# Gate products of an mLSTM block: from two column groups of 64 to four of 32

## The reference

```
xn    = layernorm(x)                       # (512, 512) per sequence
q,k,v,o = xn @ Wq.T, xn @ Wk.T, xn @ Wv.T, xn @ Wog.T
i_pre = 15 * tanh((xn @ Wig.T + big) / 15) # 8 heads: input gate
f_pre = 15 * tanh((xn @ Wfg.T + bfg) / 15) # 8 heads: forget gate
# scan over the tokens, per head:
f_log = log_sigmoid(f_pre)
m_new = max(f_log + m, i_pre)
C, n  = exp(f_log + m - m_new) * (C, n) + exp(i_pre - m_new) * (k v^T, k)
h     = (q C) / max(|q n|, exp(-m_new))
y     = x + (sigmoid(o) * headnorm(h)) @ Wout.T
out   = y + gelu(layernorm(y) @ ternary(w1).T + b1) @ ternary(w2).T + b2
```

## Time and profile before

| what | value |
|---|---|
| median of three runs | 1802.89 us (1798.72 to 1803.27) |
| the profiled execution's own time | 1799.08 us |
| its span, first to last instruction | 1797.3 us |
| TensorE busy | 1750.3 us (97% of the span) |
| VectorE busy | 1374.1 us (76%) |
| ScalarE busy | 1069.2 us (59%) |
| GpSimd busy | 588.2 us (33%) |
| mean granted clock of TensorE | 0.990 of full speed |

### The profile page before, as it was taken

How to read it: one execution, slowest core, us unless ns; L and a number is a source line. 1 busy time by engine, 2 the same in 40 slices (tenths; PEclk the granted TensorE clock), 3 DMA queues, 4 the chain that set the end, 5 groups by cost and what they waited for, 6 DMA issues and landing times.

```text
span 1797.3 us, 32014 instructions
## 1 busy us (share of the span) xinstructions
PE 1750.3 (97%) x12544; PEld 875.8 (49%) x12544; DVE 1374.1 (76%) x2464; ACT 1069.2 (59%) x1801; POOL 588.2 (33%) x481
## 2 busy tenths in 40 slices
PE   5879999999999999999999999999999999999999
PEld 3454544445454444545444454444544444454555
DVE  6787878787777778877877887877778787876772
ACT  5877648374663837557383754737466483746643
POOL 1241432524234252432425143252414325242340
PEclk8899999999999999999999999999999999999999
DMA  8434133251322425142252514325142342514020
GB/s 288 168 100 111 46 100 86 54 145 32 114 54 80 119 48 150 25 121 54 54 144 48 134 29 120 66 54 145 36 126 46 98 92 54 121 28 124 1 53 24
DMA packets 233525, 156.97 MB, mean 87 GB/s; under 512 B 195088, under 2 KB 199312, under 8 KB 228256
## 3 DMA queue, kind: packets, MB, share of 16 engines
q1 hardware_dynamic: 231792, 151.79, 31.8%
q10 hardware_dynamic: 1584, 3.15, 0.5%
HBM read 90.48 MB, written 17.24 MB: 60 GB/s over the span
## 4 chain that ended last, share of the span: by engine, by line
PE 91%; DVE 3%; ACT 1%; issue 1%; POOL 1%; DMA 0%; POOLq 0%; DVEq 0%; ACTq 0%
PE pf L1986 24%; PE pf L1970 23%; PE pa L1829 20%; PE pa L1805 9%; PE psh L1829 6%; PE psh L1926 2%; PE psh L1887 1%; PE psh L1910 1%; PE pa L1796 1%; PE psh L1960 1%; PE psh L1868 1%; PE pa L1926 1%; PE psh L1843 1%; DVE kT L1468 0%; ACT dec L930 0%
## 5 line engine op out<-in xcount | busy, mean ns | idle before, releaser
L1986 PE MATMUL pf<-w2T,gT 128*128 128x512 f16 x2048 | 497.1, 379 | 0.0
L1970 PE MATMUL pf<-x2T,w1T 128*128 128x512 f16 x1920 | 422.0, 379 | 0.0
L1970 PEld LDWEIGHTS pf<-x2T,w1T 128*128 128x128 f16 x1920 | 185.4, 98 | 222.6
L1522 DVE SCALAR_TENSOR_TENSOR gT<-g,wscale,gT 128x512 f16<-128x512 f32 x240 | 212.2, 884 | 105.6 <-ACT gT L966 105.0
L1986 PEld LDWEIGHTS pf<-w2T,gT 128*128 128x128 f16 x2048 | 195.3, 97 | 176.4
L1829 PE MATMUL pa<-wT,xT 128*128 128x512 f16 x960 | 213.5, 380 | 1.0 <-ACT sig L889 0.9
L963 ACT ACTIVATE g<-pf,b1c 128x512 f32<-128x512 f32 x240 | 164.0, 683 | 75.7 <-PE pf L1970 73.5
L971 ACT ACTIVATE ktok<-kT 128x512 f32<-128x512 f32 x64 | 40.4, 631 | 260.4 <-DVE kT L1446 260.4
L966 ACT ACTIVATE gT<-g,wscale 128x512 f16<-128x512 f32 x240 | 173.3, 722 | 7.8
L1829 PE MATMUL pa<-wT,shared 128*128 128x512 f16 x768 | 176.2, 379 | 0.8 <-DMA shared<-qT 0.7
L1805 PE MATMUL pa<-xT,wT 128*128 128x512 f16 x768 | 171.3, 379 | 0.1
(11 more groups left out here) (230 smaller groups left out, 2666.5 us busy)
## 6 DMA issues: line engine op xcount, KB each, us to landing
dec<-gate_r SPq DMA_DIRECT2D x32, 1024.0 KB, 5.6
xin<-L_attn_x SPq DMA_DIRECT2D x16, 1024.0 KB, 6.2
out<-x1b SPq DMA_DIRECT2D x64, 256.0 KB, 2.2
xres<-L_attn_x SPq DMA_DIRECT2D x16, 512.0 KB, 5.9
xres<-L_attn_x SPq DMA_DIRECT2D x32, 256.0 KB, 2.9
qw<-gate_w SPq DMA_DIRECT2D x128, 48.0 KB, 5.6
gT<-L_ffn_w SPq DMA_DIRECT2D x5, 1024.0 KB, 4.8
gT<-L_ffn_w ACTq DMA_DIRECT2D x3, 1024.0 KB, 6.2
```

What stands on the lines that cost most here:

```text
L1522: nc.vector.scalar_tensor_tensor(gT[:, LO, f, :], g32[:, f % 2, :], wscale[:, W_GELU:W_GELU + 1], gT[:, HI, f, :], ALU.mult, ALU.subtract) ...
L1970: last = nc.tensor.matmul(bank, w1T[:, k, tok(f)], x2T[:, part, :, k, :], start=(k == 0 and part == HI), stop=(k == KD - 1 and part == LO))
L1986: last = nc.tensor.matmul(bank, gT[:, part, f, tok(t)], w2T[:, f, :], start=(f == 0 and part == HI), stop=(f == NF - 1 and part == LO), sk ...
```

## The change

- The gate products go to four column groups of 32 PSUM partitions, one for each depth block. The twelve matmuls stay, of 32 weight columns instead of 64. The forget gate is in columns 0 to 7 now and the input gate in columns 8 to 15 (GROWS = 16).
- There are four partial sums in place of two: ScalarE copies the last, VectorE adds three others one after the other, each waiting for the one before; the third frees the bank.
- The input gate's rows of `th` are brought to partitions 0 to 7 (`gi`) by a new transfer of 16 KB on SyncE's queue, and VectorE multiplies them by 15 there, after a new wait, in `gate_decay`; the multiplication in `gate_logs` goes.
- On SyncE's queue the store of `ge` (and its wait for ScalarE's L866) stands behind the two large `dec` transfers now, not ahead of them.
- `gate_columns` stands behind the first query product on TensorE, and behind the first query copy on ScalarE.

```diff
-    GATE_F = 32
-    GROWS = GATE_F + NH
+    GROWS = 2 * NH
+    QUAD = P // KD
...
-        wgT = sb("wgT", [P, KD, 2, P // 2], F16)
+        wgT = sb("wgT", [P, KD, 2, QUAD], F16)
...
             def gate_rows(b):
+
+                sp.wait_ge(tanh_ok, at(b, 1, 1))
+                sp.dma_start(gi, th[NH:GROWS, :]).then_inc(i_loaded, 16)
                 sp.wait_ge(r_ok, at(b, 1, 1))
                 sp.dma_start(gate_r[b], th[0:NH, :]).then_inc(r_stored, 16)
-                sp.wait_ge(gate_act, at(b, 5, 4))
-                sp.dma_start(gate_w[b], ge[:, 0:LATE]).then_inc(w_stored, 16)
...
                     sp.dma_start(dec[:, g * H4:(g + 1) * H4, :],
...
+                sp.wait_ge(gate_act, at(b, 5, 4))
+                sp.dma_start(gate_w[b], ge[:, 0:LATE]).then_inc(w_stored, 16)
                 sp.wait_ge(w_stored, at(b, 16, 16))
...
-                nc.scalar.activation(th, pa[P // 2:P // 2 + GROWS, pa_bank(b, U_GATE), :], ACT.Copy).then_inc(gate_lo, 1)
+                nc.scalar.activation(th, pa[3 * QUAD:3 * QUAD + GROWS, pa_bank(b, U_GATE), :], ACT.Copy).then_inc(gate_lo, 1)
...
                     keys(b, 1)
+                    queries(b, 0)
                     gate_columns(b)
-                    queries(b, 0, 1)
+                    queries(b, 1)
...
             def gate_sum(b):
 
+                bank = pa_bank(b, U_GATE)
                 dve.wait_ge(gate_lo, at(b, 1, 1))
-                nc.vector.tensor_tensor(th, pa[0:GROWS, pa_bank(b, U_GATE), :], th,
-                                        ALU.add).then_inc(pa_free[pa_bank(b, U_GATE)], 1)
+                nc.vector.tensor_tensor(th, pa[2 * QUAD:2 * QUAD + GROWS, bank, :], th, ALU.add).then_inc(gate_part, 1)
+                dve.wait_ge(gate_part, at(b, 2, 1))
+                nc.vector.tensor_tensor(th, pa[QUAD:QUAD + GROWS, bank, :], th, ALU.add).then_inc(gate_part, 1)
+                dve.wait_ge(gate_part, at(b, 2, 2))
+                nc.vector.tensor_tensor(th, pa[0:GROWS, bank, :], th, ALU.add).then_inc(pa_free[bank], 1)
...
-                nc.vector.tensor_scalar(gi, th[0:NH, :], CAP, None, ALU.mult)
-                nc.vector.tensor_scalar(gf, th[GATE_F:GROWS, :], CAP, 0.0, ALU.mult, ALU.min)
+                nc.vector.tensor_scalar(gf, th[0:NH, :], CAP, 0.0, ALU.mult, ALU.min)
...
+                dve.wait_ge(i_loaded, at(b, 16, 16))
+                nc.vector.tensor_scalar(gi, gi, CAP, None, ALU.mult)
                 dve.wait_ge(gate_arg, at(b, 3, 3))
...
-                for k in range(KD // 2):
-                    for n, (ws, xs) in enumerate(PARTS):
-                        for half, rows_of in enumerate((slice(0, P // 2), slice(P // 2, P))):
-                            kc = 2 * k + half
-                            last = nc.tensor.matmul(bank[rows_of, :], wgT[:, kc, ws, :], xT[:, xs, :, kc, :],
-                                                    start=(k == 0 and n == 0), stop=(k == KD // 2 - 1 and n == 2))
+                for n, (ws, xs) in enumerate(PARTS):
+                    for k in range(KD):
+                        last = nc.tensor.matmul(bank[k * QUAD:(k + 1) * QUAD, :], wgT[:, k, ws, :], xT[:, xs, :, k, :],
+                                                start=(n == 0), stop=(n == 2), skip_group_check=True)
...
                 for n in range(HG):
                     features(b, U_K + n, C_QK + QK + n * P)
                     prepare(USES_O[n + 2])
-                gate_columns(b)
                 for n in range(HG):
                     features(b, U_Q + n, C_QK + n * P)
+                    if n == 0:
+                        gate_columns(b)
```

More of the change, by code:

```diff
@@ L254, in block_program @@
         gate_lo, tanh_ok = sem("gate_lo"), sem("tanh_ok")
+        gate_part, i_loaded = sem("gate_part"), sem("i_loaded")
         gate_arg = sem("gate_arg")
@@ L452, in _ @@
                     sp.wait_ge(s_const, 1)
[L453 to L456, removed]
+                    sp.dma_start(th[0:NH, :], Wfg).then_inc(s_wload[4], 16)
+                    sp.dma_start(th[NH:GROWS, :], Wig).then_inc(s_wload[4], 16)
+                    sp.dma_start(gate_bias[0:NH, :], bfg.unsqueeze(1)).then_inc(s_bias, 16)
+                    sp.dma_start(gate_bias[NH:GROWS, :], big.unsqueeze(1)).then_inc(s_bias, 16)
             sp.dma_start(gcol[:, :], gamma.rearrange("h v -> (h v)").rearrange("(k p) -> p k", p=P),
@@ L1295, in gate_minus @@
                     dve.wait_ge(hoT_loaded[T - 1], at(b, 16, 0))
-                nc.vector.tensor_scalar(ge, th[GATE_F:GROWS, :], CAP, None, ALU.mult).then_inc(gate_arg, 1)
+                nc.vector.tensor_scalar(ge, th[0:NH, :], CAP, None, ALU.mult).then_inc(gate_arg, 1)
                 dve.wait_ge(gate_arg, at(b, 3, 1))
```

## The result

The changed kernel takes 1804.74 us (median of 20 runs, 1802.52 to 1807.96); the kernel before, run beside it on the same chip, 1801.78 us (20 runs). The ratio is 1.0021, 95% interval 1.0014 to 1.0027: 3.8 us slower, which is also the distance of the means (1805.19 and 1801.37 us); the medians lie 3.0 apart. The 3.8 us are inside the predicted range, but I had forecast no change, and the interval excludes none. The profiled execution has a span of 1802.6 us, against 1797.3 before.

The account below looks back on a forecast made before the run. In steady blocks TensorE's queue alone was taken to bound the kernel. 1799.1 - 1.0 (steady blocks) + 0.7 (block 0) = 1798.8 profiled, 1802.6 against the runs' median; own range 1798 to 1807, wider range 1796 to 1814.

Parts of the forecast that it names:

- The gate products: Twelve matmuls on TensorE: four column groups side by side take 0.77 us instead of 1.42, a gain of 0.65.
- The sums: VectorE's three dependent sums make TensorE wait at `project(b, 3)`: 0.07 us gain left per block, 1.0 over 15 blocks.
- the 0.4 to 0.6 that I had named as a sign: TensorE's wait for VectorE's last sum, some 0.4 to 0.6 us in each of 15 blocks, if the forecast was right.
- VectorE's later work and `gate_columns`: VectorE's chain after the sums: r about 0.8 us later; `gate_columns`, done 0.1 us late behind a query product, costs 0.
- The store of `ge`: On SyncE's queue behind `dec`: lands at 1010.9; first query copy at 1011.6 leaves the output gate 0.3 us slack, cost 0.
- The second rival: The store of `ge` behind `dec` holds up the queries: 0.7 us a block, 10.5 in all, 1813 us; chance 0.12.
- The transposing transfer: On SyncE's queue, lands at 1021.6 before the first `up` product's weight load at 1022.15: slack 0.5 us, cost 0.
- The rival: The transposing transfer is late for the first `up` product: 1.0 us a block, 1818 us; chance 0.10.
- block 0: The first block, where TensorE waits for others: VectorE's two added sums cost 0 to 1.4 us once, taken as 0.7.
- "Cost 0": The new transfer of the input gate: some 4 us from issue to use against 1.40 for a small store, cost 0.

Follow-up runs that it names:

- e4: The changed kernel with the store of `ge` ahead of `dec` again and token tile 1's value product ahead of tile 0's: 1795.98 us, ratio 0.9973.
- e6: e4 with ScalarE's first key copy ahead of its token copies: 1792.92 us, ratio 0.9955 to the kernel before.
- e9: e1 with `gate_columns` back ahead of both query products, on TensorE and ScalarE: 1810.09 us, ratio 1.0042.
- e1: The changed kernel with the store of `ge` back ahead of the `dec` transfers: 1800.54 us, ratio 0.9999 to the kernel before.
- e2: The kernel before with only the store of `ge` moved behind the `dec` transfers: 1802.31 us, ratio 1.0005.
- e3: The changed kernel with the value product of token tile 1 moved ahead of that of tile 0: 1804.56 us, ratio 1.0020.
- after: The changed kernel itself, with the whole change and no further edit: 1804.74 us, ratio 1.0021 to the kernel before.
- e10: The kernel before with tile 1's value product first, the key copy first and `gate_columns` behind the first query product: 1801.86 us, ratio 1.0006.
- e7: e6 with block 0's transfer of the input gate issued by ScalarE instead of SyncE: 1792.08 us, ratio 0.9952.

## Why the prediction was wrong, point by point

**The gate products: right.** Forecast 0.77 us, measured 0.76 (e4, e6). Three steps of 0.216 are 0.65; the other 0.11 were there with two groups too (1.42 - 1.30). The Trainium skill's page TensorE: Matmul & The Clock Gate, Part 3, gives 2.38 times for three groups, from which I had estimated 0.9; here four groups are nearer to their ideal than that. My reason for leaving that figure aside did not hold, though: L1868 at 17 ns instead of 27 shows that its products overlap, but 27 / 17 is only 1.6 times, and I had no row for what one such float32 product costs alone.

**The sums: right in size.** Forecast were 0.07 us a block left over and a period of 106.2 to 106.3; it is 106.21. The sums step by 0.72 (991.36, 992.08, 992.80) and end 3.74 us behind `project(b, 2)`, forecast 3.7. The wait for the last sum is 0.2 us a block, not the 0.4 to 0.6 that I had named as a sign, because TensorE has already lost time just before it. This I had not seen: the value product waits as well, 0.16 us in most blocks, since it takes the bank of `project(b, 2)`, which L1489 frees. It costs nothing, because the next product waits for the sums anyway. This agrees with the rule cited from the Trainium skill (TensorEngine Tiling (Array Packing), PSUM Bottleneck): the products got faster, the emptying of the bank did not, and e4 and e6 give the time back once another product stands in between.

**VectorE's later work and `gate_columns`: right.** r is stored 0.7 us later (15.47 us behind the gate products against 14.80), forecast 0.8, and `gate_columns` costs nothing where the change put it. e9 shows what the move is worth.

**The store of `ge`: right.** The `qw` transfers, which wait for it, go out 24.05 us behind the gate products (1013.72 - 989.67); forecast 1010.9 - 986.35 = 24.55. The query copy and the first output-gate product weren't held up: no such wait is in the list. The second rival, 0.12, did not come.

**The transposing transfer: wrong.** This is the step that failed: "I put it at 5 us of issuing and 1.3 to land: 1021.6 ... Slack 0.5 us, cost 0". The issue came 0.8 us earlier than forecast (28.14 behind the gate products, against 28.95), the landing took longer. Transfers issued from 1011.5 to 1026 and from 1436 to 1451 us in the changed kernel (us from issue to landing):

```profile
x2T<-gT SPq DMA_TRANSPOSE x1, 7.3
```

```profile
q8 instruction: 1, 0.02, 0.4%
q14 instruction: 1, 0.01, 0.1%
...
x2T<-gT SPq DMA_TRANSPOSE x1, 8.7
```

7.3 instead of 6.3 makes 35.4 behind the gate products, where I had 35.25: for the ordinary block the slack was right, 0.3 us for 0.5. But the transfer does not always take 7.3. In ten blocks it took 7.1 to 7.3; in the five that were late it took 8.0 to 8.7, and a slack of 0.3 us can't hold that. Before, it took 8.0 to 10.6 over fifteen blocks and was never late, since it was issued 3.9 us earlier. I had read that number in one block only and took a slack that was smaller than the spread for a cost of nothing. The rival was there, with 0.10 and a price of 1.0 us in every block; what came was a quarter of that on average, 3.5 us over 15 blocks. With this term at its measured size my sum would have been -1.0 + 3.5 + 0.7 = 3.2, against 3.8 measured. e1, in which these waits are gone, gives 4.0 us back (1.0021 against 0.9999).

What makes single transfers longer the traces show in part. In each of the last three late blocks a transfer of instructions (16 KB, q8) lies within the transposing transfer, and shortly after it the DMA nearly stands still for 1 us. Stretches of the transfer of 8.45 us shown above (last two columns: DMA share and GB/s):

```profile
1553.00:1554.50 1.50, 1.50 (x9) 0.68 (x7) 1.24 (x8) 1.50 (x6) 0.08 (x1) 1.00 1.30 272
1554.80:1555.80 1.00, 1.00 (x6) 0.47 (x5) 0.34 (x1) 1.00 (x4) 0.63 (x1) 1.00 0.06 6
1556.00:1557.90 1.90, 1.75 (x9) 0.58 (x6) 1.79 (x5) 1.90 (x8) 0.00 (x0) 1.00 1.22 276
```

In the changed kernel, e2 and e3 together, ten of 45 transposing transfers have such a q8 transfer within them, and these took 8.3 to 9.0 us; the other 35 took 7.1 to 7.8, but for three of 8.0 and 8.1. Two of those three are the other two late blocks: in one, the DMA moved 30 GB/s from 169.9 to 170.9 us with no instruction transfer beside it; in the other, issued at 805.04, a smaller one (q14) lay at the start. So the lateness goes with the q8 transfers in three blocks of five. It also repeats: in all twelve profiles the longest transposing transfer of the fifteen lies in one of the last four blocks and has a q8 transfer within it. That the one causes the other isn't shown: no run moved or removed the instruction transfers.

**Two steps that I had overlooked.** First, the path through L1489 has no slack left: in the fourth period VectorE begins the residual 0.4 us late for no reason that the profile shows, and TensorE waits 0.5 us instead of 0.2. It is 0.35 us in after and in e1. Before, such a delay would have lain within the 0.9 us ahead of `project(b, 3)`. Chain of the changed kernel:

```profile
457.72 0.40 issue
458.12 0.76 DVE xres L1489
```

Second, block 0. I had "0 to 2 x 0.71", took 0.7 and gave the new transfer "Cost 0". In block 0 its cover is missing:

```profile
40.28 0.41 DVE L1330 TENSOR_SCALAR sig<-sig 8x512 f32<-8x512 f32 x1 [0.93 <-DMA sig<-qT]
```

With it the weight transposes behind VectorE's chain (L1710) start at 46.88 instead of 45.45. The profile then has block 0 longer by 2.3 us in all; the granted clock was lower too, 0.88 against 0.90 of full speed from 50 to 100 us and 0.87 against 0.91 from 100 to 140, so more of that time ran at 1.2 GHz. A single profile can't size this term: the second gate products begin at 136.1 us before and at 138.35 in e10, whose block 0 has neither sums nor transfer. e4 and e6 run the same instructions up to that point, yet from the first gate products to the second it took 114.7 us in e4 and 117.6 in e6; the granted clock from 100 to 136 us was 0.91 in e4 and 0.76 in e6. At the same 0.91 it is 113.7 before and 114.7 in e1 and e4, some 0.9 longer. From the ratios, with the steady part taken off, I get: for e6 -8.1 + 15 x 0.655 = 1.7, and for the changed kernel 3.8 - 3.0 = 0.8, each uncertain by over 1 us. The size of block 0's term stays open, between 0 and some 2 us.

## What to carry to other kernels

A shortened product pays only if the next taker of its bank isn't waiting for the engine that empties it; look for another product to put between, then for the next wait behind that one (here value tile, store, key copy), and the whole gain comes through: 0.9955 where the change itself gave 1.0021. Two delays that are free each by itself (the store's place, 1.0005; the longer chain with the old place, 0.9999) can use up one slack together. A slack must be held against the spread of the transfer over all blocks and not against one block; one that is smaller than the spread has a price.

## What the runs showed of the hardware beyond that

- Four column groups of 32 run side by side: twelve float16 products of 512 columns take 0.76 us, against 1.42 in two groups of 64 and 2.59 of full width.
- A store of 12 KB behind two transfers of 1 MB in the same queue took 4.8 to 5.0 us from issue to landing (4.97 in the chain from 1540 us), where it took some 1.4 us ahead of them.
- A transposing transfer of 1 MB landed 7.1 to 7.3 us after its issue in ten blocks of the changed kernel, and 8.3 to 8.7 us in the three in which a 16 KB transfer of instructions lay within it.
- Issuing one transfer of 16 KB took ScalarE 1.24 us in e7; SyncE took 0.67 to 0.76 us for the same one in e6.
